# Gathers of node rows in a GNN layer: written-out issue, indices read in place, waits by halves of a step

## The reference

```python
h = relu(layernorm(x))                                   # 50000 x 128
m = relu(concat(h[src], h[dst], edge_attr) @ Wm1 + bm1)  # 25000 x 128
m = relu(m @ Wm2 + bm2)
agg = segment_sum(m, dst, 50000)
u = relu(concat(h, agg) @ Wu1 + bu1)
out = x + h + (u @ Wu2 + bu2)
```

## Time and profile before

| | us |
|---|---|
| median of 3 runs | 946.89 (946.84 to 947.41) |
| the profiled execution | 952.33 |
| its span, first to last instruction | 950.6 |
| edge stage | 0 to about 665 |
| busy in the span: PE, DVE, ACT, POOL | 751.0, 696.0, 608.5, 566.0 |

### The profile page before, as it was taken

The page is one execution under the profiler, slowest core; times in us unless marked ns, Lnnn a source line. Parts: engine busy times, 40 slices in busy tenths (PEclk is TensorE's granted clock), DMA queues, the critical chain, the costliest instruction groups (busy, mean ns, idle before and its releaser), DMA issues. The chain is left out here.

```text
span 950.6 us, 19507 instructions
## 1 busy us (share of the span) xinstructions
PE 751.0 (79%) x3158; PEld 453.1 (48%) x3159; DVE 696.0 (73%) x2407; ACT 608.5 (64%) x1384; POOL 566.0 (60%) x829
## 2 busy tenths in 40 slices
PE   0687768767877778877887776886799999999998
PEld 0344334333433334433443433453457788777776
DVE  3866756666677666776667567766499999998887
ACT  0666556556656565665665566655567788988986
POOL 6656655656566555665556555654198766655453
PEclk9988888889789897889887899988899999999999
DMA  6254445445545455545553454447305799999999
GB/s 158 67 178 158 151 154 175 157 127 178 176 157 168 141 176 165 169 148 161 177 176 129 153 176 155 162 150 232 133 12 176 230 319 335 351 341 349 355 360 328
DMA packets 99726, 184.55 MB, mean 194 GB/s; under 512 B 15101, under 2 KB 16512, under 8 KB 99700
## 3 DMA queue, kind: packets, MB, share of 16 engines
q1 hardware_dynamic: 46084, 80.64, 25.4%
q10 hardware_dynamic: 41072, 77.93, 23.5%
q0 software_dynamic: 12544, 25.72, 10.5%
HBM read 107.25 MB, written 76.98 MB: 194 GB/s over the span
## 5 line engine op out<-in xcount | busy, mean ns | idle before, releaser
L246 POOL DMA_INDIRECT xg<-x_in,ends_now x392 | 386.1, 985 | 142.9 <-issue 130.1
L511 PE MATMUL bank<-ht,w_uh 128*128 128x512 f32 x196 | 146.1, 837 | 114.2 <-ACT ht L441 68.8
L644 POOL TENSOR_TENSOR low<-msgs,high 128x128 fp32r<-128x128 f32 x303 | 152.8, 521 | 73.3 <-ACT high L724 70.1
L309 DVE BATCH_NORM_STATS2 bn<-xg 128x6 f32<-128x128 f32 x392 | 80.6, 278 | 132.4 <-DMA xg<-x_in,ends_now 132.3
L673 DVE TENSOR_SCALAR hot<-node,dst_f,minus_base 128x512 fp32r<-128x512 f32 x229 | 131.2, 616 | 23.2 <-issue 16.3
L777 PE MATMUL bank<-hot,low 128*128 128x512 f32 x303 | 136.4, 450 | 12.2 <-POOL low L644 6.5
L429 ACT ACTIVATE zn<-xn,shift,rstd 128x128 f32<-128x128 f32 x343 | 141.6, 483 | 1.6 <-DVE rstd L348 1.2
L511 PEld LDWEIGHTS bank<-ht,w_uh 128*128 128x128 f32 x196 | 42.6, 249 | 199.6 <-issue 180.1
L436 ACT ACTIVATE ht<-bank 128x512 f32<-128x512 f32 x196 | 109.2, 593 | 30.3 <-PE bank L504 26.1
L778 PE MATMUL bank<-hot,high 128*128 128x512 f32 x303 | 120.8, 399 | 0.0
L504 PE MATMUL bank<-ident,xg 128*128 128x128 f32 x392 | 64.8, 298 | 61.1 <-issue 37.0
(11 more groups left out here) (77 smaller groups left out, 1165.7 us busy)
## 6 DMA issues: line engine op xcount, KB each, us to landing
hu_scratch<-ht ACTq DMA_DIRECT2D x49, 512.0 KB
xh_scratch<-xh_o ACTq DMA_DIRECT2D x49, 512.0 KB
hu_i<-hu_scratch SPq DMA_DIRECT2D x98, 256.0 KB
xh_i<-xh_scratch SPq DMA_DIRECT2D x98, 256.0 KB
out<-xh_o SPq DMA_DIRECT2D x97, 256.0 KB, 4.3
xn<-x_in ACTq DMA_DIRECT2D x44, 512.0 KB
xg<-x_in,ends_now POOLq DMA_INDIRECT x392
edge<-edge_t_in ACTq DMA_DIRECT2D x45, 64.0 KB
```

The costliest lines, as they stand in the source:

```text
L246: pool.indirect_dma_start(xg[:, slot, t, :], None, x, bass.IndirectOffsetOnAxis(ap=ends_now[:, slot8, t:t + 1], axis=0)).then_inc(s_xg[slo ...
L511: pe.matmul(p_hu[:], w_uh[:], ht[:, slot % 2, 2 + n, :], start=True, stop=True).then_inc(s_hus, 1)
L644: return pool.tensor_tensor(low[:, at, :], msgs[:, k, :], high[:, at, :].bitcast(F32), ALU.subtract)
```

## The change

The gathers of all 49 steps are written out on GpSimd in straight code, with constant counts in the waits. The indices are read from `ends_all` directly; the ring `ends_now`, its copies and `s_cp` go. Each slot has two landing semaphores, one for each four gathers. The first four gathers of step s go out when the first four of step s - 1 have landed, the second four when the second four of s - 1 have. The wait for the transposes of step s - 4 stays. VectorE waits for the two halves separately in `stat_of_ends`.

```diff
-        s_xg = [sem(f"ends_gathered{i}") for i in range(4)]
-        s_cp = sem("ends_copied")
+        s_xg = [[sem(f"ends_gathered{i}_{half}") for half in range(2)] for i in range(4)]
...
-                pool.tensor_copy(ends_now[:, 0:4], ends_all[:, 0:4, :]).then_inc(s_cp, 1)
-                pool.wait_ge(s_cp, 1)
-
-                def body(s, slot8, use8):
-                    slot = slot8 % 4
-                    if at_least(s, 4):
-                        pool.wait_ge(s_tr, 4 * (s - 3) - 2)
-                    if at_least(s, 1):
-
-                        pool.wait_ge(s_xg[(slot8 - 1) % 4], 128 * (2 * use8 + (slot8 - 1) // 4 + 1))
-                    if at_least(s, 4):
-                        pool.wait_ge(s_cp, 8 * use8 + slot8 - 2)
-                    if below(s, STEPS - 4):
-                        pool.tensor_copy(ends_now[:, (slot8 + 4) % 8, :], ends_all[:, s + 4, :]
-                                         if isinstance(s, int) else ends_all[:, bass.ds(s + 4, 1), :]).then_inc(s_cp, 1)
+
+                for s in range(STEPS):
+                    slot, use = s % 4, s // 4
+                    if s >= 4:
+                        pool.wait_ge(s_tr, 4 * (s - 4) + 2)
                     for t in range(8):
+                        if t % 4 == 0 and s >= 1:
+
+                            of, half = s - 1, t // 4
+                            pool.wait_ge(s_xg[of % 4][half], 64 * (of // 4 + 1))
                         pool.indirect_dma_start(
                             xg[:, slot, t, :], None, x,
-                            bass.IndirectOffsetOnAxis(ap=ends_now[:, slot8, t:t + 1], axis=0)).then_inc(s_xg[slot], 16)
-                    if not at_least(s, 1):
+                            bass.IndirectOffsetOnAxis(ap=ends_all[:, s, t:t + 1], axis=0)).then_inc(s_xg[slot][t // 4], 16)
+                    if s == 0:
...
-                run_steps(pool, STEPS, 8, STEPS - 4, 8, body)
...
                 def stat_of_ends(s, slot, use):
-                    dve.wait_ge(s_xg[slot], 128 * use + 128)
                     for t in range(8):
+                        if t % 4 == 0:
+                            dve.wait_ge(s_xg[slot][t // 4], 64 * use + 64)
                         ins = dve.bn_stats(bn[:, slot % 2, t, :], xg[:, slot, t, :])
                     ins.then_inc(s_stat, 1)
```

More of the change, by code:

```diff
@@ L135, in build @@
             ends_all = sb("ends_all", [P, STEPS, 8], I32, on=one)
-            ends_now = sb("ends_now", [P, 8, 8], I32, on=one)
             dst_i = sb("dst_i", [P, ET + SPARE], I32, on=one)
```

## The result

The changed kernel took **983.53 us** (median of 4 runs, 977.14 to 985.77), the kernel before 947.15 beside it: ratio 1.0372, 95% interval 1.0321 to 1.0422. The forecast was 932.5 (907 to 949). The profiled execution took 977.14 us, its span is 975.4, 24.8 above the span before. 36.4 us lie between the medians; the other 11.6 are between executions (the profiled one of after was the fastest of its four, that of before 5.2 above its median), and no trace shows them.

The account below looks back on a forecast made before the run. Two nearly equal loops, gathers (13.15 us) and load (12.80), were taken to bound the edge step, the load mostly last. Terms -3.1, -11.3 and 0 gave -14.4 us: 936.2 on the profiled span, 932.5 against the median; range 907 to 949.

Parts of the forecast that it names:

- What bounds the kernel: Edge stage, 13.45 us a step: gather loop 13.15 us and load loop 12.80 side by side, the load mostly ending last.
- A, the start: First bodies, where only gathers can hold VectorE: its waits go and `pair` of body 4 comes earlier, -3.1 us.
- B, the late bodies: Seven bodies where `pair` waits for gathers: 42.1 us from load issue to `pair` become 30.8, -11.3 us.
- C, where the gathers lie: Gathers move 2.2 us earlier in each step: slower loads and earlier load issue cancel, 0 (bounds -39 to +22).
- Rival 1, the short load loop: Steady edge steps: load issue comes early in nearly every body, 12.6 us a step, 907 us in all; chance 0.22.
- Rival 2: Edge-stage loads: continuous gathers add 0.5 us to each of 43 loads, 954.5 us in all; chance 0.13.
- (1): POOL: no copies, eight gathers in a row at 1.25 to 1.30 us, then 2 to 3 us idle, ended by TensorE's transposes.
- (2): VectorE: no gather wait worth naming; the wait before `pair` for the load grows from 1.7 to about 4 us.
- (3): Edge-stage step: `pair` to `pair` at most 13.4 us everywhere, none at 14.5 to 15.
- (4): `pair` to load issue (9.1 us) plus issue to `pair` (4.3): above 13.45 loads pay, near 12.6 the short loop holds.
- (5): The second stage, from 700 us on, keeps its length.
- runs ahead until it meets the other wait: POOL in the gather loop: issues a step's eight gathers in 10.4 us, below 13.45, until held by the transposes' wait.

Follow-up runs that it names:

- g1: Kernel before, with ScalarE issuing the node and edge load later, after copying the messages: 963.37 us, ratio 1.0215 to the kernel before.
- k1: Changed kernel, load issued right after the square root, POOL waiting for all eight previous gathers in steps 1 to 4 only: 926.49 us, ratio 0.9806.
- g4: Kernel before, with the node and edge load issued early, right after the square root: 919.74 us, ratio 0.9766.
- f2: Kernel before with nothing changed, traced on the second kind of machine: 972.13 us, ratio 1.0001.
- h2: Changed kernel, but in steps 1 to 7 POOL waits for all eight gathers of the step before: 914.27 us, ratio 0.9407.
- h3: Changed kernel, load issued right after the square root, POOL waiting for all eight previous gathers in steps 1 to 7: 827.07 us, ratio 0.8517.

## Why the prediction was wrong

- **What bounds the kernel** held on A: g1 pays for a later issue. That the load loop was bounding by so little was luck of that kind of machine. The mean issue of 9.13 us, which I took for a fact of the code, was in part a held hop: the relu of the destination rows starts 0.65 us behind their transposes on A (over 0.8 in 15 of 43 steps), 0.36 on B, where the issue stands at 8.46.
- **A, the start: -3.1 forecast, +25.1 measured.** This step decided the sign. The sum counted when gathers land, and took it that POOL running ahead costs the others nothing. The runs showed 32 gathers without a stop during which other engines wait 2 to 11 us for late increments (up to 18 in k1). No row of before shows more than eight gathers in a row without a stop, so the trace could not price it, and I gave it no bound above. On B, where nothing is held, it measured -2.7.
- **B, the late bodies: -11.3 forecast.** They went on A: issue to `pair` is 4.62 us at most and 4.17 on the mean, 185.7 / 43 = 4.32 before. The 43 sum to 179.2 us for 185.7, a gain of 6.5. The term was sized too high, for the ordinary load got slower, 4.15 us in the median for 4.02. The mechanism is shown by g4 and f2, and on B it is worth 58.7 us.
- **C, where the gathers lie: 0 forecast, +8.4 measured on A** (401.0 us from `pair` to issue summed over the 43, 392.6 before). With B's -6.5 that is the +1.8 of the steady part. The bounds held (-39 to +22). The reason given for the upper one, loads slowed by gathers, was not it: the end of the group of gathers moved away from the destination rows' hop, as I wrote, and onto the source rows' hop, one us earlier in the same chain, which I had not looked at. There TensorE starts 1.24 us behind the fourth tile on the mean of the 43 steps (0.54 before), always waiting for it.
- **Rival 1, the short load loop (907, chance 0.22)**, is what B shows in the step: 8.27 + 4.21 = 12.47 us, for 8.4 + 4.2 written. That the total of 903 lies near it too is luck, for the kernel before takes 24 us more there and the gain is 68, not 40. Rival 2 (954.5) had the sign of A and not its cause: loads did not pay 0.5 us. The rule on taking turns that stood beside term C ("DMA: Bandwidth & Descriptors" of the Trainium skill, on queues, rings and completion order) made it 0.3 us a step, an estimate; the median load paid 0.13, while the 4.55 us of a last gather beside a load on B agree with it.
- **The signs named in advance**: (1) right, copies gone, POOL idle 3.58 us at 404.48 behind TensorE's transposes (2 to 3 written). (2) right, 182.8 us of load wait. (3) half right, none above 14.24, but 26 of 43 above 13.4. (4) issue 9.33 and 4.17, sum 13.49: above 13.45 as rival 2 has it, but by the issue and not by the load. (5) right, 2 us shorter.

The faulty step was thus one sentence that cost nothing in the sum, "runs ahead until it meets the other wait", and a range that took its bounds from steady steps only.

## What to carry over

A producer that is freed runs ahead, and what it does to the others while it does so is a term of its own: look for the longest stretch in the old trace in which it runs without a stop, and where the new one is longer, give that term a bound on the dear side. Before a transfer is costed, ask whether its issue point is a fact of the code or of a late semaphore; an issue that waits for nothing belongs early in its queue (here 0.7 us a step in the kernel before and 1.4 in the changed one on A, 2.0 on B from h2 to h3; the whole change gives 1.6 on B). And a small ratio measured on one machine may have the other sign on the next: compare only beside the old kernel.

## What was new about the hardware

- Gathers issued at 1.25 us without a stop come with late semaphore increments of VectorE and TensorE on some machines, from some 13 to 15 us into the row: waits of 2 to 18 us between two instructions of one engine, over some 5 us after POOL's last gather. POOL's own waits for gathers pass meanwhile, and the DMA engines carry 53 GB/s. On other machines the same code shows nothing of it.
- With eight gathers and a stop the same machines still record single increments 1.15 us late (42 of 43 steps), the others 0.01 us.
- With a load of 512 KB issued within 0.27 us of the last gather's start, VectorE has its rows 4.55 us after that start, 2.71 where the load is elsewhere.
- The two kinds differ by some 2.5% on the kernel before and the other way round by 8% on the changed one.
